# The windowed-attention loop of a fused block: look-ahead for turned pieces, another order at its end, and constant matmuls behind the first scores

## The chip, the core and the metric

The kernel runs on one core of a Trainium2 chip. The metric is the device time of one execution in microseconds (us). Engines are TensorE (PE in the profile; PEld is its weight load), VectorE (DVE), ScalarE (ACT), GpSimd (POOL) and SyncE (SP). PSUM is the memory of 8 banks of 512 float words per partition into which TensorE writes.

## What is computed

The reference is a chain of four blocks over x of shape (2, 512, 128): a hyperbolic attention block with feed-forward part (A), a quantised attention (B), a causal attention with an image token (C), and two layers of windowed attention with a gated feed-forward part (D). The change touches D alone. Its core, once for each of the 2 layers:

```python
h = shift_token(x)                      # half of the channels moved by one token
q, k, v = split(h @ wqkv)               # 8 heads of 64
q = l2norm(q) * qs
k = l2norm(k) * ksc
q, k = rotary_xpos(q, k)                # two products and a sum per element
o = local_attention(q, k, v)            # windows of 64, each sees itself and the one before
x = x + o @ wo
h = shift_token(x)
mu = h.mean(-1, keepdims=True)
var = h.var(-1, keepdims=True)
h = (h - mu) / jnp.sqrt(var + 1e-05) * lg + lb
h = h @ w1 + b1
a, g = jnp.split(h, 2, axis=-1)
x = x + (a * jax.nn.gelu(g, approximate=False)) @ w2 + b2
```

## The kernel before

Each engine's program is written out by hand, in order, and engines wait for one another's semaphores; an engine never passes an instruction that waits. The 1,024 tokens are T = 8 tiles of 128 (TB = 4 to a batch). In D a layer starts with the projection to queries, keys and values (L1762), which ScalarE copies (L674) and squares (L679); VectorE sums the squares (`norms`, L1255) and rotates the heads pair of tiles by pair of tiles (`rotate`, L1278 to L1283; keys also get their scale, L317). Keys and queries then have to be turned: a *piece* is a pair of tiles p by a group i of two 128-column blocks (i = 0, 1 keys, 2, 3 queries). TensorE turns it by four transposes (`turn_piece`, L1774) into one of two spare slots in the score banks, ScalarE copies it to SBUF (`turned_qk`, L668) and counts `qk_ev`.

The loop over u runs through UNITS = 16 units for a layer, a unit being half of the heads of one tile. In unit u TensorE turns a piece, makes the scores (`s_d`, L1799 a mask, L1810 and L1812 the products), turns the probabilities of unit u - 2 (L1859) and multiplies those of unit u - 3 with the values (`pv_d`, L1824). VectorE reduces the scores to a maximum (L1351), makes the bias (L1357) and, between, runs two steps of the rotations of later tiles (`later_rotations`, by `next(rest)`) and the reciprocal of the sums of unit u - 1 (L1369). ScalarE makes four exponentials (L698), copies the turned piece, copies the turned probabilities of unit u - 2 (L710) and, in odd units up to 11, a finished output tile (L714; later tiles are VectorE's, `put_o`, L288). GpSimd scales the probabilities (L460) and lays out values (L449, L451).

Pieces of p = 0 are turned ahead of the loop; unit u turns piece u % 4 of pair u // 4 + 1, and units 4p to 4p + 3 need all four pieces of pair p. The projection of the outputs by wo (`project_o`, L1781) of tiles 0 to 3 stands in units 12 and 13, two to a unit, of tiles 4 to 7 at the end of the loop. VectorE adds them to the residual (`add_o`, L758), sends and receives the shifted half (L1232, L1237; TensorE L1790, L1791) and normalises (`less_mean`, `variance`, `normalise`, L1313, L770, L1327); ScalarE takes the roots (`roots_d`, L662, behind a table load), and `turn_e` (L1419) and `hidden` (L1893) start the feed-forward part. `keep_busy(n)` (L1437) issues n matmuls of a constant into a bank that nobody reads then.

The waits of the unit on TensorE, which the change rewrites:

```python
if u >= 2:
    pe.wait_ge(sem["expD"], 4 * (U - 1))
    pe.wait_ge(sem["qk_ev"], UNITS * l + min(u + 3, UNITS))
if u % 4 == 0:
    pe.wait_ge(sem["qk_ev"], UNITS * l + u + 4)
if u < UNITS - 4:
    turn_piece(u // 4 + 1, u % 4, u % 2)
```

## Time and profile before

| | |
|---|---|
| median of 3 runs | 790.16 us (789.87 to 793.35) |
| the profiled execution | 788.48 us, its span 786.7 us |
| TensorE busy | 626.8 us, 80% |
| VectorE busy | 542.5 us, 69% |
| ScalarE busy | 499.9 us, 64% |
| GpSimd busy | 239.5 us, 30% |
| chain that ended last | PE 43%, DVE 30%, ACT 15%, issue 9% |

No engine is busy all the time; which of them bounds a stage differs from stage to stage. In the rows below a line of the order of time has start, duration, engine, source line and operation, what is written and read, the number of instructions merged, and in brackets how long the engine sat idle before and what it waited for. A float32 matmul counts as two instructions in some rows, so 8 of L1781 are one output projection. Times are from the start of the span.

### The profile page before, as it was taken

How to read it: one execution, taken by the hardware profiler on the slowest of the kernel's cores; microseconds unless marked ns; L12 is line 12 of the kernel's file. 1: busy time of each engine (PE TensorE's matmuls, PEld its weight loads, DVE VectorE, ACT ScalarE, POOL GpSimd, SP SyncE). 2: the span in 40 equal slices, each digit the busy share in tenths (PEclk: the TensorE clock that was granted, in tenths of full speed). 3: DMA queues.
4: the chain of work that ended last, by engine and by line, in shares of the span. 5: the costliest groups of instructions: out<-in, count | busy, mean ns of one | idle time of the engine just before them, and what ended most of it. 6: DMA issues, size and time to landing. Idle time of an engine off the chain costs nothing.

```text
span 786.7 us, 13264 instructions
## 1 busy us (share of the span) xinstructions
PE 626.8 (80%) x4802; PEld 377.4 (48%) x4802; DVE 542.5 (69%) x1119; ACT 499.9 (64%) x1187; POOL 239.5 (30%) x237
## 2 busy tenths in 40 slices
PE   7679986767789988966889798695878779578776
PEld 3312222354356655644555455543656544356654
DVE  7783328747899889767787877569754457984444
ACT  4459997661778878715477666385576439667642
POOL 5030006011789978970200000000554100055400
PEclk9779999998555555595599999896599999678999
DMA  8400000000000000000000000000000000000000
GB/s 277 157 1 1 1 1 1 0 1 0 1 2 1 1 2 2 1 1 0 1 1 2 1 1 2 1 1 0 2 2 2 1 0 0 1 2 2 1 1 27
DMA packets 9204, 9.88 MB, mean 13 GB/s; under 512 B 2890, under 2 KB 7988, under 8 KB 9012
## 3 DMA queue, kind: packets, MB, share of 16 engines
q1 hardware_dynamic: 9140, 9.04, 3.5%
q8 instruction: 39, 0.64, 0.3%
q14 instruction: 25, 0.20, 0.1%
HBM read 8.51 MB, written 0.52 MB: 11 GB/s over the span
## 4 chain that ended last, share of the span: by engine, by line
PE 43%; DVE 30%; ACT 15%; issue 9%; POOL 2%; DMA 1%; ACTq 0%; DVEq 0%; POOLq 0%
PE ps L1691 4%; PE ps L1431 4%; PE ps L1594 4%; DVE s_nmB L1086 4%; PE ps L1674 3%; ACT arena L571 3%; PE ps L1581 3%; PE ps L1711 3%; PE ps L1502 2%; ACT dev L698 2%; PE ps L1474 2%; PE ps L1893 2%; PE ps L1781 2%; ACT arena L674 2%; DVE s_nmD L1351 2%
## 5 line engine op out<-in xcount | busy, mean ns | idle before, releaser
L415 POOL TENSOR_SCALAR arena<-arena,s_rB,s_zpu 128x512 uint8<-128x512 f32 x128 | 115.9, 943 | 35.2 <-DVE s_rB L1059 34.7
L609 ACT ACTIVATE arena<-ps,s_nmB 128x512 f32<-128x512 f32 x128 | 86.6, 683 | 31.7 <-DVE s_nmB L1086 31.2
L631 ACT ACTIVATE arena<-ps,s_nmx 128x512 f32<-128x512 f32 (+3 forms) x128 | 60.7, 527 | 50.2 <-DVE s_nmx L1184 49.7
L1086 DVE TENSOR_REDUCE s_nmB<-ps 128x2 f32<-128x1024 f32 x64 | 77.3, 1216 | 6.9 <-PE ps L1581 6.6
L449 POOL COPY arena<-arena 64x512 f32<-64x512 f32 x16 | 13.0, 814 | 220.9 <-PE ps L1774 219.0
L1179 DVE TENSOR_REDUCE s_nmx<-ps 128x1 f32<-128x512 f32 (+3 forms) x128 | 56.6, 483 | 21.5 <-PE ps L1677 21.0
L571 ACT ACTIVATE arena<-ps 128x1024 f32<-128x1024 f32 x64 | 60.9, 1026 | 6.5 <-PE ps L1486 6.5
L1594 PE MATMUL ps<-cst,arena 128*128 128x128 f32 x256 | 61.0, 416 | 1.7 <-POOL arena L415 0.8
L1437 PE MATMUL ps<-ones 128*128 128x512 f16 x134 | 40.9, 457 | 24.2 <-ACT s_rn L562 3.6
L1581 PE MATMUL ps<-staged 8*128 8x512 f16 x128 | 46.7, 585 | 11.7 <-ACT arena L609 10.9
L1594 PEld LDWEIGHTS ps<-cst,arena 128*128 128x128 f32 x256 | 48.7, 218 | 14.6 <-POOL arena L415 8.0
L1691 PE MATMUL ps<-cst,arena 128*128 128x128 f32 x320 | 46.9, 301 | 8.7 <-issue 5.2
L1351 DVE TENSOR_REDUCE s_nmD<-ps 128x4 f32<-128x512 f32 x32 | 22.1, 691 | 45.7 <-PE ps L1812 30.0
L698 ACT ACTIVATE sq<-ps,s_nbD,s_dq 128x128 f32<-128x128 f32 x64 | 28.4, 454 | 33.1 <-DVE s_nbD L1357 33.1
L1691 PEld LDWEIGHTS ps<-cst,arena 128*128 128x128 f32 x320 | 39.6, 155 | 11.9 <-issue 9.6
L1762 PE MATMUL ps<-w_d,uT 128*128 128x512 f32 x96 | 42.3, 595 | 3.5 <-ACT uT L520 1.4
L1774 PE MATMUL ps<-cst,arena 128*128 128x128 f32 x128 | 26.6, 351 | 22.1 <-ACT arena L668 11.2
L1674 PE MATMUL ps<-staged 51*128 51x512 bf16 (+3 forms) x128 | 33.0, 332 | 9.8 <-ACT arena L631 8.6
L460 POOL TENSOR_TENSOR sq<-sq,s_rsD 128x512 f32<-128x512 f32 x16 | 22.4, 1400 | 51.1 <-DVE s_rsD L1369 51.1
L1437 PEld LDWEIGHTS ps<-ones 128*128 128x128 f16 x134 | 13.4, 110 | 49.2 <-issue 8.8
L698 ACT ACTIVATE dev<-ps,s_nbD,s_dq 128x128 f32<-128x128 f32 x64 | 28.5, 457 | 13.0 <-DVE s_nbD L1357 13.0
L1502 PE MATMUL ps<-arena 128*32 128x512 f32 x256 | 35.8, 633 | 1.0 <-ACT arena L571 1.0
(337 smaller groups left out, 1510.4 us busy)
## 6 DMA issues: line engine op xcount, KB each, us to landing
w_d<-in_wqkv SPq DMA_DIRECT2D x2, 768.0 KB
vec<-in_vec SPq DMA_DIRECT2D x1, 1200.0 KB, 10.8
vec<-in_vec SPq DMA_DIRECT2D x1, 960.0 KB, 8.0
w_h<-in_w SPq DMA_DIRECT2D x2, 341.0 KB
x_tok<-in_x SPq DMA_DIRECT2D x1, 512.0 KB, 4.0
arena<-in_w_f SPq DMA_DIRECT2D x2, 256.0 KB, 7.7
rope<-in_rope SPq DMA_DIRECT2D x1, 512.0 KB, 9.2
w_do<-in_wo SPq DMA_DIRECT2D x2, 256.0 KB
```

Of the source, the lines that this page charges most:

```text
L415: nc.gpsimd.tensor_scalar(u8[:, n % 4, j // 2, :, 2 * (j % 2)], prob[:, n % 2, j * 512:j * 512 + 512], sm("rB", 8)[:, c:c + 1], sm("zpu", ...
L571: nc.scalar.activation(prob[:, n % 2, half * 1024:half * 1024 + 1024], ps[:, 2 * half:2 * half + 2, :], ACT.Exp, scale=HD ** -0.5).then_in ...
L609: nc.scalar.activation(prob[:, n % 2, j * 512:j * 512 + 512], ps[:, j, :], ACT.Exp, bias=sm("nmB", 8)[:, c:c + 1], accum_out=sm("sumB", 8) ...
L631: nc.scalar.activation(probC[:, n % 2, at(qt):at(qt) + w], ps[:, bank, col:col + w], ACT.Exp, bias=nmx[:, TB * b + qt, h:h + 1]).then_inc( ...
L698: nc.scalar.activation(prob_d(U)[:, k, :], scores_d(u)[:, j, a, :], ACT.Exp, scale=sm("dq8", 8 * T)[:, h:h + 1], bias=sm("nbD", 16)[:, c:c ...
L1086: free(V.tensor_reduce(sm("nmB", 8)[:, c:c + 2], ps[:, 2 * half:2 * half + 2, :], X, ALU.max, negate=True), "maxB")
L1179: ins = V.tensor_reduce(nmx[:, TB * b + qt, h:h + 1], ps[:, bank, col:col + P * (qt + 1)], X, ALU.max, negate=True)
L1437: M(ps[:, 5, :], ones16[:, :], ones16[:, 0:1].to_broadcast([P, 512]), start=True, stop=True)
L1581: ins = M(ps[:, j, :], staged[r, G % 2, qt * P:qt * P + P], staged[r, G % 2, 512:1024], start=True, stop=True)
L1594: ins = nc.tensor.transpose(ps[:, 4 + i, c:c + P], codes[:, m % 4, i, c:c + P], ident)
L1674: M(o, stb[r, G % 2, qt * P:qt * P + P], stb[r, G % 2, 512:512 + w], start=(qt > 0), stop=False)
L1691: ins = nc.tensor.transpose(ps[:, 3 + bank, c:c + P], probC[:, n % 2, a:a + P], ident)
```

## The change

Four things are altered, all in the D loop.

1. Pieces are turned five ahead: five pieces before the loop (`FIRST_PIECES`, the fifth is piece 0 of pair 1), and unit u turns piece u + 5. The wait for ScalarE's copies is the same in each unit, u + 4, and the extra wait at u % 4 == 0 is gone. VectorE makes one rotation step more ahead of the loop, and the factors of the second half (`factors(1)`) come behind the next step.
2. Eight constant matmuls follow the scores of unit 0.
3. The projections of tiles 0 to 3 stand in unit 11 (two), 12 and 13 (one each), and VectorE's additions with them.
4. At the end, projections 4 and 5 stand in u = 17, behind the turned probabilities of unit 15 and the values of unit 14; 6 and 7 in u = 18, behind `turn_e(0)`. ScalarE loads the table of the root at u = 16, by an activation of one column.

The diff, cut to its core:

```diff
-        primed = sb("primed", [P, 12])
+        primed = sb("primed", [P, 16])
...
+        FIRST_PIECES = ((0, 2), (0, 3), (0, 0), (0, 1), (1, 0))
...
+        PROJECTED_AT = {11: (0, 1), 12: (2,), 13: (3,)}
+
+        def projected_o(t):
+
+            return ps[:, (6, 7, 0, 6)[t], 256:256 + P]
...
-                            for k, i in enumerate((2, 3, 0, 1)):
-                                turned_qk(0, i, 1 - k % 2)
+                            for k, (p, i) in enumerate(FIRST_PIECES):
+                                turned_qk(p, i, 1 - k % 2)
...
-                    if u < UNITS - 4:
-                        turned_qk(u // 4 + 1, u % 4, u % 2)
+                    if u + 5 < UNITS:
+                        turned_qk((u + 5) // PIECES, (u + 5) % PIECES, u % 2)
...
+                    if u == UNITS:
+                        load_table(ACT.Sqrt)
...
                 rest = later_rotations()
                 next(rest)
+                next(rest)
...
+                        if u == 11:
+                            add_o(0, 2, ps[:, 6:8, 256:256 + P])
                         if u in (12, 13):
-                            add_o(2 * (u - 12), 2, ps[:, 6 * (u % 2), 256:512])
+                            add_o(u - 10, 1, projected_o(u - 10).unsqueeze(1))
...
-                        if u == 0:
-                            factors(1)
                         if u == 13:
                             send(0)
                     next(rest, None)
+                    if u == 0:
+                        factors(1)
...
                         if u >= 2:
                             pe.wait_ge(sem["expD"], 4 * (U - 1))
-                            pe.wait_ge(sem["qk_ev"], UNITS * l + min(u + 3, UNITS))
-                        if u % 4 == 0:
-                            pe.wait_ge(sem["qk_ev"], UNITS * l + u + 4)
-                        if u < UNITS - 4:
-                            turn_piece(u // 4 + 1, u % 4, u % 2)
-                        if u in (12, 13):
-                            for k in range(2):
-                                project_o(2 * (u - 12) + k, ps[:, 6 * (u % 2), 256 + P * k:256 + P * k + P])
-                        if u >= 14:
-                            pe.wait_ge(sem["do_ev"], 3 * l + u - 13)
+                        pe.wait_ge(sem["qk_ev"], UNITS * l + min(u + 4, UNITS))
+                        if u + 5 < UNITS:
+                            turn_piece((u + 5) // PIECES, (u + 5) % PIECES, u % 2)
+                        for t in PROJECTED_AT.get(u, ()):
+                            project_o(t, projected_o(t))
+                        if u >= 13:
+                            pe.wait_ge(sem["do_ev"], 4 * l + u - 12)
                         if u == 14:
                             shift_rows(0)
                         s_d(u)
+                        if u == 0:
+                            keep_busy(8)
...
-                    if u >= UNITS:
-                        if u == UNITS:
-                            pe.wait_ge(sem["expD"], 4 * (U - 1))
-                            pe.wait_ge(sem["lnsq"], B * l + 1)
-                        t = TB + u - UNITS
-                        project_o(t, ps[:, 0, P * (t - TB):P * (t - TB) + P])
-                project_o(T - 1, ps[:, 0, 3 * P:4 * P])
...
+                    if u > UNITS:
+                        if u == UNITS + 1:
+                            pe.wait_ge(sem["expD"], 4 * (U - 2))
+                        else:
+                            turn_e(0)
+                        for t in range(2 * u - 2 * UNITS + 2, 2 * u - 2 * UNITS + 4):
+                            project_o(t, ps[:, 0, P * (t - TB):P * (t - TB) + P])
```

Next, what stands in a row on the engines at three places. In these rows a name behind `waits` is the semaphore.

The first place is VectorE's entry into the loop, from the last three sums of squares on. Before (L1278 to L1283 are the steps of a rotation, L1351 and L1357 belong to a unit's scores, L762 and L773 are the factors):

```order
L1255 TENSOR_REDUCE s_dss<-arena 128x16 [waits d_sq] x3
L1278 TENSOR_TENSOR o_tok<-arena,ropeL 128x1024
L1351 TENSOR_REDUCE s_nmD<-ps 128x4 [waits sD,dve_step]
L1357 TENSOR_TENSOR s_nbD<-s_nmD,s_dq 128x4 [waits dve_step]
L762 TENSOR_SCALAR s_dn<-s_dn 128x64 [waits d_n]
L773 RECIPROCAL s_dn<-s_dn 128x64 [waits dve_step]
L762 TENSOR_SCALAR s_dq<-s_dn 128x32 [waits dve_step]
L1280 TENSOR_TENSOR staged<-arena,ropeL 128x16x32 [waits d_dn]
L1281 TENSOR_TENSOR staged<-arena,ropeL 128x16x32 [waits dve_step]
L1283 TENSOR_TENSOR arena<-o_tok,staged 128x2x512 [waits dve_step]
L1351 TENSOR_REDUCE s_nmD<-ps 128x4 [waits sD,ropeQ]
```

The same place in the changed program (L1287 to L1292 the rotation, L1361 and L1369 the scores, L771 and L782 the factors):

```order
L1264 TENSOR_REDUCE s_dss<-arena 128x16 [waits d_sq] x3
L1287 TENSOR_TENSOR o_tok<-arena,ropeL 128x1024
L1289 TENSOR_TENSOR staged<-arena,ropeL 128x16x32 [waits dve_step]
L1290 TENSOR_TENSOR staged<-arena,ropeL 128x16x32 [waits dve_step]
L1361 TENSOR_REDUCE s_nmD<-ps 128x4 [waits sD,dve_step]
L1369 TENSOR_TENSOR s_nbD<-s_nmD,s_dq 128x4 [waits dve_step]
L1292 TENSOR_TENSOR arena<-o_tok,staged 128x2x512
L771 TENSOR_SCALAR s_dn<-s_dn 128x64 [waits d_n,ropeQ]
L782 RECIPROCAL s_dn<-s_dn 128x64 [waits dve_step]
L771 TENSOR_SCALAR s_dq<-s_dn 128x32 [waits dve_step]
L1287 TENSOR_TENSOR o_tok<-arena,ropeL 128x1024 [waits d_dn]
L1361 TENSOR_REDUCE s_nmD<-ps 128x4 [waits sD,dve_step]
```

The two half-width products now stand ahead of the first reduction, and the first product of the next rotation ahead of the second.

The second place is TensorE from the scores of unit 0 to those of unit 1. Before (L1812 scores, L1774 a piece turned, L1799 the mask of unit 1):

```order
L1812 MATMUL ps<-arena 64x128 x2
L1774 MATMUL ps<-cst,arena 128x128 [waits keys0]
L1774 MATMUL ps<-cst,arena 128x128 x3
L1799 MATMUL ps<-dmask,identb 128x256 x2
```

The same place changed (L1824 scores, L1449 the constant matmuls, L1786 a piece turned, L1811 the mask):

```order
L1824 MATMUL ps<-arena 64x128 x2
L1449 MATMUL ps<-ones 128x512 x8
L1786 MATMUL ps<-cst,arena 128x128 [waits ropeQ,qk_ev]
L1786 MATMUL ps<-cst,arena 128x128 x3
L1811 MATMUL ps<-dmask,identb 128x256 x2
```

Unit 1's turn is now of rotated queries, so it waits for `ropeQ`, and unit 1's scores stand behind it.

The third place is the end of the loop on TensorE, from the turned probabilities of unit 14. Before (L1859 probabilities, L1824 values, L1781 projections, L1419 the normalised tiles turned, each row ahead of an equal one with x3 or x7 left out by dots):

```order
L1859 MATMUL ps<-cst,dev 128x128 [waits ptcD,normD]
...
L1824 MATMUL ps<-arena 64x64 [waits mixD,ptcD]
...
L1781 MATMUL ps<-w_do,arena 128x128 [waits o_D1,lnsq,expD]
...
L1859 MATMUL ps<-cst,dev 128x128 [waits ptcD,normD]
...
L1824 MATMUL ps<-arena 64x64 [waits o_D1,mixD,ptcD]
...
L1781 MATMUL ps<-w_do,arena 128x128 [waits o_D1]
...
L1824 MATMUL ps<-arena 64x64 [waits mixD,ptcD]
...
L1781 MATMUL ps<-w_do,arena 128x128 [waits o_D1]
...
L1781 MATMUL ps<-w_do,arena 128x128 [waits o_D1]
...
L1419 MATMUL ps<-cst,o_tok 128x128 [waits lnD]
```

The same place changed (L1875 probabilities, L1841 values, L1793 projections, L1431 the normalised tiles):

```order
L1875 MATMUL ps<-cst,dev 128x128 [waits ptcD,normD]
...
L1841 MATMUL ps<-arena 64x64 [waits mixD,ptcD]
...
L1875 MATMUL ps<-cst,dev 128x128 [waits ptcD,normD]
...
L1841 MATMUL ps<-arena 64x64 [waits o_D1,mixD,ptcD]
...
L1793 MATMUL ps<-w_do,arena 128x128 [waits o_D1,expD]
...
L1793 MATMUL ps<-w_do,arena 128x128 [waits o_D1]
...
L1841 MATMUL ps<-arena 64x64 [waits mixD,ptcD]
...
L1431 MATMUL ps<-cst,o_tok 128x128 [waits lnD]
...
L1793 MATMUL ps<-w_do,arena 128x128 [waits o_D1]
...
L1793 MATMUL ps<-w_do,arena 128x128 [waits o_D1]
```

The probabilities of unit 15 have no projection ahead of them any more, and the turn of the normalised tiles stands ahead of the last two projections.

## Rows read from the trace of the kernel before

**Rows 1.** The page's granted clock of TensorE, in 40 slices of the span.

```profile
PEclk9779999998555555595599999896599999678999
```

**Rows 2.** Windows: stretch, busy us of PE, PEld, DVE, ACT, POOL, clock.

```profile
core 0: us, PE busy (x) PEld busy (x) DVE busy (x) ACT busy (x) POOL busy (x), PEclk, DMA share, GB/s
544.90:563.40 18.50, 11.29 (x115) 8.75 (x116) 15.69 (x26) 10.80 (x39) 7.07 (x5) 0.50 0.00 1
...
582.10:597.50 15.40, 12.69 (x205) 10.13 (x206) 3.80 (x13) 12.18 (x42) 5.97 (x7) 0.99 0.00 1
```

**Rows 3.** Order of time, VectorE: score reductions; the last two are layer 1's.

```profile
544.88 0.69 DVE L1351 TENSOR_REDUCE s_nmD<-ps 128x4 f32<-128x512 f32 x1
...
557.09 0.69 DVE L1351 TENSOR_REDUCE s_nmD<-ps 128x4 f32<-128x512 f32 x1
563.37 0.69 DVE L1351 TENSOR_REDUCE s_nmD<-ps 128x4 f32<-128x512 f32 x1 [2.22 <-PE ps L1812]
568.25 0.69 DVE L1351 TENSOR_REDUCE s_nmD<-ps 128x4 f32<-128x512 f32 x1 [1.54 <-issue]
...
582.14 0.69 DVE L1351 TENSOR_REDUCE s_nmD<-ps 128x4 f32<-128x512 f32 x1 [2.38 <-issue]
...
591.00 0.69 DVE L1351 TENSOR_REDUCE s_nmD<-ps 128x4 f32<-128x512 f32 x1 [1.83 <-ACT dev L698]
597.50 0.69 DVE L1351 TENSOR_REDUCE s_nmD<-ps 128x4 f32<-128x512 f32 x1 [5.52 <-PE ps L1812]
...
608.70 0.69 DVE L1351 TENSOR_REDUCE s_nmD<-ps 128x4 f32<-128x512 f32 x1
680.12 0.69 DVE L1351 TENSOR_REDUCE s_nmD<-ps 128x4 f32<-128x512 f32 x1
...
718.10 0.69 DVE L1351 TENSOR_REDUCE s_nmD<-ps 128x4 f32<-128x512 f32 x1 [2.58 <-issue]
```

**Rows 4.** Order of time, layer 0's front: rotation steps on VectorE, TensorE's turn in unit 2.

```profile
543.63 1.21 DVE L1278 TENSOR_TENSOR o_tok<-arena,ropeL 128x1024 f32<-128x1024 f32 x1
...
546.71 0.69 DVE L1280 TENSOR_TENSOR staged<-arena,ropeL 128x512 f32<-128x512 f32 x1
...
548.16 1.22 DVE L1283 TENSOR_TENSOR arena<-o_tok,staged 128x1024 f32<-128x1024 f32 x1
...
549.53 1.09 PE L1774 MATMUL ps<-cst,arena 128*128 128x128 f32 x4 [5.19 <-DVE arena L1283]
```

**Rows 5.** Order of time, TensorE: constant matmuls in block A, then units of layer 0.

```profile
36.36 3.57 PE L1437 MATMUL ps<-ones 128*128 128x512 f16 x8 [3.56 <-ACT s_rn L562]
...
561.50 0.63 PE L1799 MATMUL ps<-dmask,identb 128*128 128x256 bf16 x2
...
566.39 0.64 PE L1799 MATMUL ps<-dmask,identb 128*128 128x256 bf16 x2
...
579.46 1.09 PE L1774 MATMUL ps<-cst,arena 128*128 128x128 f32 x4 [2.07 <-ACT arena L668]
...
583.44 0.66 PE L1774 MATMUL ps<-cst,arena 128*128 128x128 f32 x4
```

**Rows 6.** Order of time, TensorE at unit 12: two output projections.

```profile
594.52 2.02 PE L1781 MATMUL ps<-w_do,arena 128*128 128x128 f32 x16 [1.69 <-ACT arena L668]
```

**Rows 7.** Order of time, layer 0's end of the loop, TensorE and ScalarE.

```profile
612.12 1.09 ACT L710 ACTIVATE arena<-ps 128x512 f32<-128x512 f32 x2
...
613.43 2.08 PE L1781 MATMUL ps<-w_do,arena 128*128 128x128 f32 x8
...
615.30 1.06 PE L1859 MATMUL ps<-cst,dev 128*128 128x128 f32 x4
...
616.40 0.60 ACT L710 ACTIVATE arena<-ps 128x512 f32<-128x512 f32 x1 [3.19 <-PE ps L1859]
617.02 1.28 ACT L662 ACT_TABLE_LOAD   x1
...
621.40 1.16 PE L1781 MATMUL ps<-w_do,arena 128*128 128x128 f32 x8 [1.47 <-DVE arena L288]
...
623.69 1.98 PE L1893 MATMUL ps<-uT,w_h 128*128 128x512 f32 x4 [0.69 <-ACT uT L512]
```

17 lines of the change are left out of this document (8 added, 9 removed).

## The prediction

> **What bounds the kernel now.** I read the page first for the granted TensorE clock over the span, then the D stages (two layers, some 540 to 624 us and 676 to 760 us) as a table of windows, then the list of the score reductions on VectorE, one in each unit, and last the order of time on all engines around the longest gaps between them.
>
> The page's clock line shows 5 to 6 tenths of full speed in two places, one of them the middle of each D loop's front [rows 1]. The windows say where: 0.50 (1.2 GHz) over the first four units of layer 0 and 0.99 (2.4 GHz) from unit 8 on [rows 2]. The reductions pace the loop [rows 3]. From unit 0 to unit 8 they take 37.26 us in layer 0 and 37.98 us in layer 1; from unit 8 to unit 15, 26.56 us in layer 0. Three units are long: the step to unit 4 is 6.28 us (563.37, after 557.09), to unit 8 6.54 us, to unit 12 6.50 us, against some 3 to 5 for the others. In each VectorE sits idle before the reduction (2.22, 2.38 and 5.52 us), though before the other units it is busy with the rotations until about 580 us.
>
> The reason for the three is one wait. At u = 4, 8, 12 TensorE needs the piece that was turned in the unit before and that ScalarE copies only behind that unit's four exponentials. At unit 8 TensorE is idle 2.07 us until that copy and then runs at the low level (1.09 us for four transposes) [rows 5]; at unit 12 it is idle 1.69 us and then spends 2.02 us on two output projections before the scores [rows 6].
>
> **Part A, units 0 to 8.** Pieces are turned five ahead, so the copy that unit 4 or 8 needs is made one unit of ScalarE earlier. The cover for all of it is VectorE: its rotation work is the same, so the ceiling is its idle time in this stretch, 2.22 + 1.54 + 2.38 = 6.1 us in layer 0 [rows 3]. The front costs something against it. I lay it out in layer 0's times.
>
> VectorE does the two half-width products (0.69 us each) ahead of reduction 0, so this moves from 544.88 to 546.3; ropeQ of pair 1 (the 1.22 us addition) is done at 548.4 instead of 549.4, since the factors now come behind it [rows 4]. TensorE has two turns and the scores of unit 0 done at about 542.9 (one turn, about 1.1 us, later than now: hidden, the reduction comes at 546.3). The eight constant matmuls take 3.57 us at the low level [rows 5], until 546.5; they end before 548.4, so they delay nothing, and cost nothing unless ropeQ came over 1.9 us earlier. Then TensorE turns piece (1,2), which unit 1's scores stand behind: 2.6 us at the low level, 1.5 at the high one, so reduction 1 falls at 550.6 to 551.1 where it was at 549.4. VectorE loses at most 0.5 us by this, because it has done one more rotation step by then.
>
> Reductions 2 and 3 follow at VectorE's own pace of some 3.6 us (554.2, 557.8). Here the new order has a wait of its own: piece (2,0) is turned in unit 3, not 4, and needs the scaled keys of pair 2, which VectorE finishes at about 556.5. Scores 3 are then ready at 558.1 (high level) or 559.4 (low). Scores 4 need transposes, values, one turn and scores behind these: 3.2 us at the high level, 4.9 at the low one, the latter being the distance of two units in the rows (561.50 to 566.39) [rows 5]. So reduction 4 falls between 562 and 564.4 instead of 563.4: a gain of 1.4 or a loss of 1.0 there. From unit 4 on VectorE's rotations set the pace. A unit of it is reduction and product (0.9), a reciprocal (0.2) and two rotation steps of 1.2 us, or 1.4 to 1.9 where the step is the two half-width products beside GpSimd's work: about 4.2, 4.0, 3.6, 4.0 us for units 3 to 6, then the loop's own 3.3; unit 8 comes at 577 (clock high throughout) to 579.3 (low until about 565), against 582.1. That is 2.8 to 5.1 us in layer 0, and 0.7 more in layer 1, whose front is that much longer now. I take 3.7 for each layer: the matmuls fill about 3.5 us of a gap of 5.19 [rows 4], but leave two idle stretches of 2 to 3 us, so part of the front stays at the low level.
>
> The page TensorE: Matmul & The Clock Gate of the Trainium skill (table of the two states) says that an idle engine returns to 1.2 GHz and that sustained work is needed for 2.4 GHz. By this rule the two gaps that remain would leave most of the front low and part A at its lower end, 2.8 instead of 3.7 us. The trace agrees in part: after 2.07 us idle the engine is low at 579.46, and after work without a gap it is high again at 583.44 [rows 5].
>
> **Part B, units 8 to 15.** The four projections of the first half (1.0 us each) move from two and two in units 12 and 13 to two, one, one in units 11 to 13. In layer 0's times: behind the values product that ends at 589.4 stand now projections 0 and 1 (2.0) in place of one turn (0.5), so scores 11 are ready at 592.4 and reduction 11 comes 1.45 us later than its 591.00. Then transposes 0.6, values 0.6, one projection 1.0, scores 1.0: reduction 12 at 595.65 instead of 597.50 [rows 3]. The copy that unit 12 waited for is long there. That is 1.85 us by unit 12, and unit 13 has one projection where it has two now, some 0.95 more: 2.8 us in each layer by unit 15. VectorE's additions follow the projections: one of 256 columns (0.4 us) in unit 11, one of 128 in each of 12 and 13 in place of 256; I count them at nothing, as ScalarE has until 596.6 to copy output tile 3, on which projection 3 waits. Gain 2.8 us in each layer; bounds 1.7 (only the wait of [rows 6] is saved) and 3.2.
>
> **Part C, the tail.** Now [rows 7]: ScalarE copies two units until 613.21, TensorE does projection 4 at the low level (2.08) before the transposes of unit 15 (615.30), ScalarE's last copy ends at 617.0, the table load takes 1.28 us, and the root, VectorE's normalising, the last output copy, projection 7 (621.40) and the copy of the turned tiles follow one another up to the hidden products at 623.69. After: the transposes of unit 15 stand directly behind the values product, at 613.43 to 614.4. The table load and its one-column activation run from 613.2 to 614.75 while ScalarE would be idle (3.19 us now), the last copy ends at 615.3, the root at 615.5, normalising and addition at 617.6. TensorE meanwhile: values 615.2, projections 4 and 5 at mixed levels until 617.85, the last values 618.5, the turn of the normalised tiles 619.1, the output copy on VectorE until 619.25 beside it, projections 6 and 7 until 621.1. The hidden products start at 621.1 instead of 623.69: 2.6 us, in each layer, and all behind them moves along. Bounds: 1.0 (low level for all four projections) and 3.2.
>
> **Sum.** 2 x (3.7 + 2.8 + 2.6) = 18.2 us. The profiled execution took 788.48 us (span 786.7); it becomes 770.3. The median of the runs lies 1.7 above the profiled one, so 772.0.
>
> **The rivals.**
> (1) The front gives nothing: the clock stays at the low level through units 1 to 7, each then 4.9 us on TensorE against VectorE's 4.0, and piece (2,0) waits for its keys. For it: the two remaining gaps. Against it: those units hold the same work in less idle time than now. 2 x (2.8 + 2.6) = 10.8 saved: 779.4.
> (2) The table load costs more than its row. The page ScalarE: Activation LUTs of the Trainium skill (What ACT_TABLE_LOAD costs) adds a drain of 1380 ns to the 1283 ns of the load. Worked from the rows as a mechanism of this kernel: should ScalarE be blocked about as long again as the load, the last copy comes 1.35 us later and part C shrinks to 1.25: 774.7. Against it: the load at 617.02 begins 0.02 us behind the copy and the root follows it at once.
> (3) Only the tail gains, because another wait takes the place of the copies' (projections 0 and 1 in unit 11 fully exposed, ropeQ late for each turn): 5.2 saved, 785.
> (4) Slower: the clock. Units 8 to 15 run at 0.99 now. With the waits gone TensorE waits in smaller portions; should this stretch fall to the low level, a unit costs 4.9 us [rows 5] instead of 2.95 (582.14 to 591.00 for three) [rows 3], or a little more in the odd units: about 1.8 more. Ten such units use up the whole gain of 18.2, and all 16 in both layers give 29 more: 801. Against it: its busy share rises by the change, and it kept 0.99 while 18% idle (12.69 us busy of 15.40) [rows 2].
>
> **Chances.** As forecast 0.60 (own range 767 to 777); (1) 0.20; (2) 0.08; (3) 0.07; (4) 0.05. The range of 765 to 781 holds the first three and the upper bounds of A to C. Three runs that spread by some 3 us tell 0.5% (4 us) from no change. Faster by over 0.5%: 0.91; within: 0.05; slower: 0.04.
>
> **What the new profile would show.** Steps to units 4, 8 and 12 of 4.5 us or less; no wait of TensorE's turn for ScalarE's copy at units 8 and 12; reduction 0 to reduction 8 in 32 to 33 us, reduction 8 to 15 in about 23.8; the table load in the middle of the last three copies; the first hidden product some 9.0 us after ScalarE begins the copy of unit 13's probabilities, where it is 11.6 now (612.12 to 623.69). Wrong it would be by a clock of 0.50 past unit 5, by a long wait for ropeQ or keys before a turn in units 1 to 5, or by ScalarE's last copy waiting for the load.

## The result, and the profile after

| | before | changed |
|---|---|---|
| median of 4 runs each | 790.01 us (788.75 to 793.35) | 777.47 us (776.55 to 778.91) |
| the profiled execution | 788.48 us, span 786.7 us | 776.55 us, span 774.7 us |

The changed kernel takes 0.9836 of the time (95% interval 0.9803 to 0.987), 12.5 us less. The forecast was 772.0 (765 to 781): the sign and the range hold, the size was 5.5 us too good.

The page of the changed kernel: the span, the busy times, and the granted clock of TensorE in 40 slices.

```profile
span 774.7 us, 13302 instructions
PE 623.8 (81%) x4818; PEld 378.4 (49%) x4818; DVE 544.4 (70%) x1121; ACT 501.3 (65%) x1189; POOL 236.1 (30%) x237
PEclk9779997899755555576589999989689899969989
```

The busy times are those of before within 3.4 us (GpSimd 236.1 after 239.5 us, the others 3.0 us or less), while the span is 12.0 us shorter: most of the gain is waiting that is gone. The slice in which layer 0's front lies (the 29th) has a 6 where it had a 5 [rows 1].

The D loop of layer 0 as windows: units 0 to 3, 4 to 7, 8 to 14, and from the last score reduction to the first hidden product (columns as in [rows 2]). A granted clock of 0.50 is called the low level of TensorE (1.2 GHz), 1.00 the high one (2.4 GHz); a value between is an average over a stretch with both.

```profile
547.80:566.00 18.20, 13.06 (x136) 9.69 (x136) 14.27 (x24) 10.39 (x38) 6.87 (x5) 0.65 0.01 1
566.00:580.60 14.60, 11.47 (x192) 8.78 (x192) 14.13 (x22) 10.24 (x37) 7.64 (x7) 0.97 0.01 3
580.60:605.60 25.00, 22.13 (x362) 17.58 (x362) 11.14 (x32) 20.43 (x75) 12.03 (x14) 1.00 0.01 2
605.60:618.60 13.00, 10.76 (x109) 9.46 (x110) 6.15 (x15) 7.49 (x18) 3.09 (x4) 0.74 0.00 1
```

The first four units have 0.65 where they had 0.50 [rows 2], and last 18.2 us where they lasted 18.5. Units 4 to 7 are the ones that became short: 14.6 us, after 18.8 (563.37 to 582.14, [rows 3]). The tail runs at 0.74.

The order of time on VectorE, score reductions 0, 3, 4, 7, 8, 9, 11, 12 and 15 of layer 0.

```profile
547.77 0.69 DVE L1361 TENSOR_REDUCE s_nmD<-ps 128x4 f32<-128x512 f32 x1
...
561.51 0.69 DVE L1361 TENSOR_REDUCE s_nmD<-ps 128x4 f32<-128x512 f32 x1 [1.95 <-PE ps L1824]
566.02 0.69 DVE L1361 TENSOR_REDUCE s_nmD<-ps 128x4 f32<-128x512 f32 x1 [0.96 <-DVE arena L1292]
...
578.21 0.69 DVE L1361 TENSOR_REDUCE s_nmD<-ps 128x4 f32<-128x512 f32 x1
580.60 0.68 DVE L1361 TENSOR_REDUCE s_nmD<-ps 128x4 f32<-128x512 f32 x1
584.64 0.69 DVE L1361 TENSOR_REDUCE s_nmD<-ps 128x4 f32<-128x512 f32 x1 [2.67 <-PE ps L1824]
...
592.07 0.69 DVE L1361 TENSOR_REDUCE s_nmD<-ps 128x4 f32<-128x512 f32 x1 [3.38 <-PE ps L1824]
595.39 0.69 DVE L1361 TENSOR_REDUCE s_nmD<-ps 128x4 f32<-128x512 f32 x1 [1.88 <-PE ps L1824]
...
605.57 0.69 DVE L1361 TENSOR_REDUCE s_nmD<-ps 128x4 f32<-128x512 f32 x1
```

The three long steps are gone: to unit 4 it is 4.51 us (was 6.28), to unit 8 2.39 (6.54), to unit 12 3.32 (6.50). Longer ones have come instead: 5.30 to unit 3, and 4.04 from unit 8 to unit 9.

Reductions turned out to be a poor mark at unit 8, so the account below uses the exponentials on ScalarE, in both kernels from the start of the last four sums of squares ahead of the loop. In the kernel before, layer 0, order of time: the sums of squares, the first exponential of unit 8, and that of unit 15.

```profile
539.12 4.60 DVE L1255 TENSOR_REDUCE s_dss<-arena 128x16 f32<-128x1024 f32 x4
...
583.07 0.46 ACT L698 ACTIVATE sq<-ps,s_nbD,s_dq 128x128 f32<-128x128 f32 x1 [2.88 <-DVE s_nbD L1357]
...
609.85 0.46 ACT L698 ACTIVATE dev<-ps,s_nbD,s_dq 128x128 f32<-128x128 f32 x1 [0.76 <-DVE s_nbD L1357]
```

The same three of the changed kernel, with ScalarE's end of unit 7 (its first exponential, the turned piece L675, the output tile L723).

```profile
540.56 4.60 DVE L1264 TENSOR_REDUCE s_dss<-arena 128x16 f32<-128x1024 f32 x4
...
579.37 0.46 ACT L705 ACTIVATE dev<-ps,s_nbD,s_dq 128x128 f32<-128x128 f32 x1 [1.69 <-DVE s_nbD L1369]
...
581.12 0.60 ACT L675 ACTIVATE arena<-ps 128x512 f32<-128x512 f32 x1
...
582.07 0.62 ACT L723 ACTIVATE arena<-ps 128x512 f32<-128x512 f32 x1
582.55 0.50 ACT L705 ACTIVATE sq<-ps,s_nbD,s_dq 128x128 f32<-128x128 f32 x1
...
606.72 0.46 ACT L705 ACTIVATE dev<-ps,s_nbD,s_dq 128x128 f32<-128x128 f32 x1 [0.76 <-DVE s_nbD L1369]
```

Reduction 8 begins at 580.60, but its exponentials only at 582.55: ScalarE is still busy with unit 7, whose own reduction came at 578.21. Its copies there stand behind the exponentials of unit 7, so an earlier reduction 8 does not bring them forward.

| from, to | before, layer 0 / 1 | changed, layer 0 / 1 | gain | forecast, a layer |
|---|---|---|---|---|
| sums of squares to exponential 8 | 43.95 / 44.67 | 41.99 / 41.83 | 1.96 / 2.84 | 3.7 (A) |
| exponential 8 to exponential 15 | 26.78 / 27.01 | 24.17 / 24.18 | 2.61 / 2.83 | 2.8 (B) |
| exponential 15 to first hidden product | 13.84 / 13.59 | 11.85 / 12.29 | 1.99 / 1.30 | 2.6 (C) |

That is 13.5 us over both layers. The span became 12.0 us shorter: the changed kernel's execution enters D's layer 0 1.44 us later (540.56 against 539.12) on code that the change doesn't touch, and the stretches between and behind the loops differ by 0.1 us together. Why the entry is later wasn't tested. All kernels of this study have the same code ahead of D, and in their fourteen profiles, of four sets of runs, the entry lies anywhere between 539.12 and 547.36 us. That spread is more than half of the whole gain, so the account above rests on the stretches inside the loops and not on the span.

The loop's end in the changed kernel, order of time on ScalarE and TensorE (L717 probabilities of units 13, 14 and 15, L478 table load and its activation, L669 root, L1875 turned probabilities, L1793 projections, L1431 normalised tiles, L1904 hidden products).

```profile
609.00 1.09 ACT L717 ACTIVATE arena<-ps 128x512 f32<-128x512 f32 x2
610.10 1.28 ACT L478 ACT_TABLE_LOAD   x1
610.70 1.12 PE L1875 MATMUL ps<-cst,dev 128*128 128x128 f32 x4
611.39 0.20 ACT L478 ACTIVATE primed<-ones 128x1 f32<-128x1 f16 x1
611.85 0.60 ACT L717 ACTIVATE arena<-ps 128x512 f32<-128x512 f32 x1 [0.26 <-PE ps L1875]
612.35 0.20 ACT L669 ACTIVATE s_std<-s_var 128x4 f32<-128x4 f32 x1
612.80 2.95 PE L1793 MATMUL ps<-w_do,arena 128*128 128x128 f32 x16
...
616.29 0.66 PE L1431 MATMUL ps<-cst,o_tok 128*128 128x128 f32 x4
616.78 1.95 PE L1793 MATMUL ps<-w_do,arena 128*128 128x128 f32 x16
618.57 1.88 PE L1904 MATMUL ps<-uT,w_h 128*128 128x512 f32 x4
```

The load is hidden: the last copy waits 0.26 us for TensorE's transposes, and these run at the low level (1.12 us for four). Projections 4 and 5 (x16) take 2.95 us where 6 and 7 take 1.95. The first hidden product comes 9.57 us after the copy of unit 13's probabilities; before it was 11.57 [rows 7].

### The profile page after: what moved, and what is told of

Same layout as the page of the kernel before. It is cut to its first block, busy times and chain, and to the rows that moved or that the text cites. A ratio compares the mean times of both kernels' runs of the same rounds, so it can differ in the third digit from the quotient of the medians.

```text
span 774.7 us, 13302 instructions
## 1 busy us (share of the span) xinstructions
PE 623.8 (81%) x4818; PEld 378.4 (49%) x4818; DVE 544.4 (70%) x1121; ACT 501.3 (65%) x1189; POOL 236.1 (30%) x237
## 4 chain that ended last, share of the span: by engine, by line
PE 45%; DVE 35%; ACT 10%; issue 8%; POOL 1%; DMA 1%; ACTq 0%; DVEq 0%; POOLq 0%
PE ps L1443 5%; PE ps L1703 4%; PE ps L1606 4%; DVE s_nmB L1095 4%; PE ps L1686 3%; PE ps L1723 3%; PE ps L1593 2%; PE ps L1793 2%; ACT arena L578 2%; PE ps L1841 2%; PE ps L1514 2%; PE ps L1486 2%; DVE s_nmD L1361 2%; PE ps L1904 2%; PE ps L1431 2%
## 5 line engine op out<-in xcount | busy, mean ns | idle before, releaser
L1449 PE MATMUL ps<-ones 128*128 128x512 f16 x150 | 43.4, 441 | 23.2 <-ACT s_rn L569 3.6
L1361 DVE TENSOR_REDUCE s_nmD<-ps 128x4 f32<-128x512 f32 x32 | 22.1, 690 | 34.1 <-PE ps L1824 29.8
L1774 PE MATMUL ps<-w_d,uT 128*128 128x512 f32 x96 | 42.3, 595 | 3.5 <-ACT uT L527 1.4
L705 ACT ACTIVATE sq<-ps,s_nbD,s_dq 128x128 f32<-128x128 f32 x64 | 28.5, 460 | 18.8 <-DVE s_nbD L1369 18.5
L705 ACT ACTIVATE dev<-ps,s_nbD,s_dq 128x128 f32<-128x128 f32 x64 | 28.5, 460 | 18.2 <-DVE s_nbD L1369 18.1
L1449 PEld LDWEIGHTS ps<-ones 128*128 128x128 f16 x150 | 15.0, 109 | 49.4 <-issue 8.9
L1786 PE MATMUL ps<-cst,arena 128*128 128x128 f32 x128 | 25.2, 343 | 13.6 <-DVE arena L1292 6.5
```

The source lines that it names most:

```text
L705: nc.scalar.activation(prob_d(U)[:, k, :], scores_d(u)[:, j, a, :], ACT.Exp, scale=sm("dq8", 8 * T)[:, h:h + 1], bias=sm("nbD", 16)[:, c:c ...
L1449: M(ps[:, 5, :], ones16[:, :], ones16[:, 0:1].to_broadcast([P, 512]), start=True, stop=True)
```

## The experiments

Kernels of one chip are compared with each other. On the first chip of the experiments the kernel before has a median of 798.04 us, on the second 793.93, on the third 797.39, where it was 790.01 in the result above; so ratios carry over better than times. "Units 0 to 8" is from reduction 0 to reduction 8 (in kernels with the look-ahead reduction 0 itself comes 1.45 us later behind the sums of squares, 7.21 us against 5.76, so this column shows them that much too good), "units 8 to 15" likewise, and "tail" from reduction 15 to the first hidden product, in layer 0 / layer 1.

| kernel | median | ratio, 95% interval | units 0 to 8 | units 8 to 15 | tail |
|---|---|---|---|---|---|
| before | 790.01 | | 37.26 / 37.98 | 26.56 / 26.78 | 14.99 / 14.74 |
| changed | 777.47 | 0.9836 (0.9803 to 0.987) | 32.83 / 32.67 | 24.97 / 24.98 | 13.00 / 13.44 |
| no constants | 782.0 | 0.9807 (0.9763 to 0.9851) | 32.83 / 31.51 | 24.99 / 24.99 | 12.78 / 12.23 |
| look-ahead only | 787.16 | 0.9874 (0.9834 to 0.9914) | 32.82 / 31.50 | 26.05 / 26.05 | 15.20 / 14.64 |
| end only | 793.57 | 0.995 (0.992 to 0.9979) | 37.28 / 36.42 | 29.53 / 26.62 | 12.29 / 12.26 |
| projections back | 784.33 | 0.9841 (0.9803 to 0.988) | 32.83 / 33.41 | 26.04 / 25.02 | 12.24 / 12.11 |
| changed, again | 778.76 | 0.9816 (0.9779 to 0.9853) | 32.81 / 32.67 | 24.98 / 24.98 | 13.00 / 13.43 |
| no constants, again | 778.97 | 0.9818 (0.9781 to 0.9854) | 32.83 / 32.60 | 24.97 / 24.38 | 13.00 / 12.12 |
| reciprocal first | 778.69 | 0.9809 (0.9769 to 0.9848) | 32.43 / 33.79 | 25.65 / 24.83 | 12.30 / 13.14 |
| 24 constants | 775.15 | 0.9769 (0.9732 to 0.9805) | 31.66 / 32.96 | 24.22 / 23.88 | 12.24 / 12.29 |
| 24 constants, again | 776.0 | 0.9742 (0.9712 to 0.9772) | 31.66 / 32.95 | 24.21 / 23.89 | 12.24 / 12.30 |
| gaps filled | 771.83 | 0.9685 (0.9659 to 0.9711) | 31.67 / 32.46 | 24.22 / 23.94 | 11.05 / 11.05 |
| gaps filled, reciprocal first | 775.68 | 0.974 (0.9711 to 0.9768) | 32.69 / 32.76 | 24.84 / 25.65 | 11.05 / 11.05 |
| constants alone | 796.85 | 0.9989 (0.9965 to 1.0014) | 37.26 / 37.65 | 29.47 / 26.98 | 14.95 / 15.39 |

My theory at the start: the look-ahead and the moved projections give what the front and the middle gain, the new end what the tail gains, and the eight constants nothing. The rival: the constants carry part of it through the clock.

### The four parts, one by one

Without the constants: the changed kernel less this edit.

```diff
-                        if u == 0:
-                            keep_busy(8)
```

> The changed kernel without its eight constant matmuls. Theory (the look-ahead and the order at the end carry the gain; the matmuls end 2.84 us before the turn that follows, and the turn still runs at 1.09 us, the low level): same as the changed kernel within 2 us, 776 to 779; reduction 4 of layer 0 at most 1.5 us later behind reduction 0 than the 18.2 us of the changed kernel. Rival (the clock of the front carries part A): units 2 to 5 stay at the low level in both layers, 2 to 3 us a layer, 781 to 784.

The look-ahead alone: the kernel before with edit 1 of the change (five pieces ahead, VectorE's entry), projections and end as they were. Its core on TensorE, with the copies on ScalarE and VectorE's entry left out:

```diff
-                        if u % 4 == 0:
-                            pe.wait_ge(sem["qk_ev"], UNITS * l + u + 4)
-                        if u < UNITS - 4:
-                            turn_piece(u // 4 + 1, u % 4, u % 2)
+                        pe.wait_ge(sem["qk_ev"], UNITS * l + min(u + 4, UNITS))
+                        if u + 5 < UNITS:
+                            turn_piece((u + 5) // PIECES, (u + 5) % PIECES, u % 2)
```

> The kernel before with the look-ahead alone: pieces five ahead, VectorE's order at the entry, no constant matmuls, projections and end as before. Theory: part A stays (3.0 and 3.9 us by unit 8 in the two layers) and unit 12 loses its wait of 1.7 us, less what unit 9 gives back (about 1.2): 8 to 9 us below the kernel before, 781 to 782. Rival (look-ahead gains only together with the constants): under 4 us, 786 or more.

The end alone: the kernel before with edit 4 (the root's table at u = 16, projections 4 and 5 in u = 17, 6 and 7 behind the turn of the normalised tiles). The new lines; the old projections that they replace are left out:

```diff
+                    if u == UNITS:
+                        load_table(ACT.Sqrt)
...
+                    if u > UNITS:
+                        if u == UNITS + 1:
+                            pe.wait_ge(sem["expD"], 4 * (U - 2))
+                        else:
+                            turn_e(0)
+                        for t in range(2 * u - 2 * UNITS + 2, 2 * u - 2 * UNITS + 4):
+                            project_o(t, ps[:, 0, P * (t - TB):P * (t - TB) + P])
```

> The kernel before with the order at the end of the loop and the early table load alone. Theory: from reduction 15 to the first hidden product 13.0 to 13.4 us instead of 15.0 and 14.7: 3.3 us in all, 786 to 787. Rival (my forecast of part C, low level only in part of the tail): 5.2 us, 785. Rival (the end of the loop starts later things that collide, or the load delays the last copy): no gain, 790.

The projections of tiles 0 to 3 back in units 12 and 13, two each, in the changed kernel (VectorE's additions go back with them).

```diff
-                        for t in PROJECTED_AT.get(u, ()):
-                            project_o(t, projected_o(t))
+                        if u in (12, 13):
+                            for k in range(2):
+                                project_o(2 * (u - 12) + k, ps[:, 6 * (u % 2), 256 + P * k:256 + P * k + P])
```

> The changed kernel with the first four projections two and two in units 12 and 13, as before. Theory (moving them spreads the same TensorE work; the gain of part B is the wait of the copy): reduction 8 to 15 takes 25 to 25.5 us instead of 24.97 and 24.98, 0.5 us a layer at most: 777.5 to 778.5. Rival (the spreading hides about 1 us a layer under ScalarE): 779 to 780.

Without the constants the time is 782.0 us, which is in the range that the rival named. But the kernel before takes 8 us more on this chip than in the result, and the ratio is 0.9807 against 0.9836: no gain of the constants shows. The next section compares the two on one chip.

The look-ahead is most of the change: alone 0.9874, and units 0 to 8 of layer 0 take 32.82 us, as in the changed kernel. By the exponentials it gains 1.95 and 3.99 us up to exponential 8, 1.53 and 1.77 from there to exponential 15, and nothing in the tail (-0.20 and 0.10): 9.1 us of the 13.5. The median is 10.9 us below that of the kernel before, where I expected 8 to 9.

The end alone gives 0.995 and a tail of 12.3 us, a gain of 2.7 and 2.5: part C at its forecast. My theory for that run (13.0 to 13.4 us) was wrong, and the rival right.

The moved projections give 1.07 and 1.06 us: with them back, exponential 8 to 15 takes 25.24 us in both layers, against 24.17 and 24.18. My theory for that run expected 0.5 at most; the rival, under which they matter, is right. (By reductions layer 1 seems to show nothing, 25.02 against 24.98, because reduction 8 comes late there: 33.41 us.)

The end alone shows one thing more, in the windows of units 8 to 15 of layer 0 and layer 1, which hold equal work.

```profile
590.40:619.90 29.50, 25.63 (x366) 20.56 (x366) 10.57 (x29) 18.86 (x69) 10.95 (x13) 0.88 0.00 1
726.50:753.10 26.60, 22.80 (x366) 18.11 (x366) 10.57 (x29) 18.86 (x69) 10.96 (x13) 0.99 0.01 2
```

The same instructions (x366) take 2.9 us more in layer 0, at 0.88 instead of 0.99. The low level lies in two places, each behind a wait for ScalarE's copy. The first is unit 8, behind a wait of 2.07 us: the step from reduction 8 to 9 is 4.15 us, where it is 2.88 in layer 1. The second is the two projections of unit 12:

```profile
604.14 3.65 PE L1783 MATMUL ps<-w_do,arena 128*128 128x128 f32 x16 [1.70 <-ACT arena L668]
```

This is 3.65 us where it is 2.02 in [rows 6], so the step to unit 12 is 8.1 us instead of 6.5. The kernel with constants alone (below) has the same 8.1. Both keep the waits of units 4, 8 and 12. In no profile of a kernel with the look-ahead does it occur (the two projections take 2.05 us in all of them). It may be part of why the kernel before has higher medians on these chips. A larger part may lie ahead of D, where nothing was changed: in the four profiles of this chip the entry is at 544.71 to 547.36 us, in the two of the result at 539.12 and 540.56. Neither is shown, as the kernel before was not profiled there.

### The constants, and the order on VectorE

The changed kernel once more, and the same without constants, on one chip.

> The changed kernel as it is, on the same chip as the next one, to compare the two with and without constants. Ratio to the kernel before 0.983 to 0.985. Steps from reduction 0 to reduction 8 of layer 0 again 32.83 us, the first product of the feed-forward part 12.1 to 13.4 us behind reduction 15.

> The changed kernel without the eight constant matmuls, a second time, beside the changed one. Theory (the constants end before anything that waits, and the clock is low again when the next turn starts): same median within 1.5 us, and reduction 0 to 8 of layer 0 32.83 us in both. Rival (they warm the front): 2 to 4 us slower than the changed kernel. Rival (they cost, by shifting the stretches of low clock to a worse place): 2 us or more faster.

They are 778.76 and 778.97 us, with runs that spread by 3 to 4 us: the eight constants give nothing that shows. Layer 0 is the same to exponential 8 with them and without (41.99 us each). In layer 1 the profiles without them are the shorter ones, 40.69 and 41.16 us against 41.83 in both profiles of the changed kernel; so if the constants do anything, they cost a little. The changed kernel's order of time on TensorE in the front says why: the constants, the turn in unit 1, the turned probabilities of unit 0, and the turn in unit 3.

```profile
544.03 3.07 PE L1449 MATMUL ps<-ones 128*128 128x512 f16 x8
...
549.94 1.08 PE L1786 MATMUL ps<-cst,arena 128*128 128x128 f32 x4 [2.84 <-DVE arena L1292]
...
557.13 1.12 PE L1875 MATMUL ps<-cst,sq 128*128 128x128 f32 x4 [2.77 <-POOL sq L467]
558.38 1.09 PE L1786 MATMUL ps<-cst,arena 128*128 128x128 f32 x4
```

They end at 547.1, TensorE sits idle for 2.84 us, and the turn behind runs at the low level (1.08 us), just as it does without them behind 5.84 us of idling. The next gap is 2.77 us, in unit 2, where TensorE waits for GpSimd's scaling, and the turn for unit 3 is low again (1.09). Scores 3 stand behind it, and VectorE waits 1.95 us at reduction 3. The scaling itself waits for the reciprocal, which stands behind a rotation step on VectorE. That is a rival to the clock as what holds the front back; so one kernel has the reciprocal ahead of the reduction, in units 1 to 7, without constants.

In the edit `rates(u)` is the reciprocal with its waits, moved into a function; units above 7 call it at the old place.

```diff
                 for u in range(UNITS + 1):
                     U = UNITS * l + u
+                    if 1 <= u <= 7:
+                        rates(u)
...
-                        if u == 0:
-                            keep_busy(8)
```

> The changed kernel without constants, and VectorE's reciprocal of unit u - 1 ahead of the reduction of unit u for u = 1 to 7 instead of behind it and a rotation step. Theory (in the front GpSimd, and behind it the turned probabilities, wait for this reciprocal: TensorE 2.77 us in unit 2 and 2.31 us in unit 6): 0.5 to 1.5 us less from reduction 0 to exponential 8 in each layer, 1 to 3 us faster than without it. Rival (the scores of units 1 and 3 wait for the piece's ropeQ and keys, which stay where they are, and VectorE sets the pace of the others): no difference, reduction 0 to 8 again 32.8 us.

And, apart from that, enough constants to fill most of both gaps.

```diff
-                        if u == 0:
-                            keep_busy(8)
+                        if u in (0, 2):
+                            keep_busy(16 if u == 0 else 8)
```

> The changed kernel with 16 constants behind the scores of unit 0 and 8 more behind those of unit 2, to fill the two gaps that the eight leave. Theory (VectorE's pace and the keys bind the front, the clock costs it 1 to 2 us): units 1 to 4 at the high level, reduction 3 behind reduction 0 by 12.5 us instead of 13.7, reduction 0 to 8 31.5 us: 2 us a layer faster at most. Rival (they hold up the turn and the scores behind them): slower by up to 3 us, reductions 1 and 3 later.

The reciprocal's place gives nothing (778.69 against 778.97): 0.4 less in units 0 to 8 of layer 0, 1.2 more in layer 1. My theory for it was wrong. The 24 constants give 3.6 us (775.15 against 778.76). Their order of time on TensorE: both groups of constants, and the rows that answer to those above.

```profile
544.99 4.81 PE L1449 MATMUL ps<-ones 128*128 128x512 f16 x16
550.89 0.63 PE L1786 MATMUL ps<-cst,arena 128*128 128x128 f32 x4 [1.10 <-DVE arena L1292]
...
553.74 1.91 PE L1449 MATMUL ps<-ones 128*128 128x512 f16 x8
...
557.57 0.65 PE L1875 MATMUL ps<-cst,sq 128*128 128x128 f32 x4 [1.91 <-POOL sq L467]
...
573.50 0.66 PE L1875 MATMUL ps<-cst,sq 128*128 128x128 f32 x4 [2.31 <-POOL sq L467]
574.71 1.11 PE L1786 MATMUL ps<-cst,arena 128*128 128x128 f32 x4
```

The turn takes 0.63 us, and the first four units of layer 0 15.95 us instead of 18.25. The last two rows show what is given back: in units 6 and 7 the gaps remain, and TensorE is at the low level in the turn at 574.7, so that of 2.30 us after four units 1.17 are left after eight. By the exponentials, as in the account above, the gain is 1.92 and 0.72 us to exponential 8 (40.07 and 41.11 us), nothing from there to exponential 15 (24.18 and 24.10), and 0.76 and 1.15 us in the tail (11.09 and 11.14): what the change promised for the tail (2.6) is there with these constants, 2.75 and 2.45.

### Filling what gaps remain

The 24 constants again beside the next two, and a kernel with 20 and 14 in the front and ten more at the loop's end, where they go to banks whose readers are done (`keep_busy` gets the bank as a second argument; that line is left out).

> The changed kernel with 16 constants behind the scores of unit 0 and 8 behind those of unit 2, a second time, beside the next two. Ratio to the kernel before 0.975 to 0.979.

```diff
                         s_d(u)
-                        if u == 0:
-                            keep_busy(8)
+                        if u in (0, 2):
+                            keep_busy(20 if u == 0 else 14)
+                    if u == UNITS - 1:
+                        keep_busy(2, 3)
...
+                    if u == UNITS:
+                        keep_busy(2, 1)
...
                         pv_d(t, u - 3)
+                    if u == UNITS - 1:
+                        keep_busy(6, 2)
```

> The changed kernel with 20 and 14 constants in the front and 2, 6 and 2 in the gaps of units 15 and 16, written to banks that nobody reads then. Theory (the low level of TensorE at the end of the loop costs part C about 1 us a layer): reduction 15 to the first product of the feed-forward part 11.0 to 11.5 us instead of 12.2 to 13.4, and the front as with 24 constants; 1.5 to 3 us faster than those alone. Rival (ScalarE's copies and VectorE's normalising set the end, not TensorE): 12.1 us or more, no difference.

The same with the reciprocal ahead of the reduction.

> The same as the kernel with the gaps filled, and the reciprocal ahead of the reduction in units 1 to 7. Theory (with the clock high the waits for GpSimd are what is left in the front: 1.91, 0.62, 1.76 and 2.31 us): reduction 0 to 8 under 31 us in layer 0, 1 us a layer faster. Rival (as in the kernel with the reciprocal alone, VectorE's own pace stays): same within 1 us.

And the constants without the change: the kernel before with 16 of them in unit 1 and 4 in unit 2, where its front has its gaps.

```diff
                         s_d(u)
+                        if u in (1, 2):
+                            keep_busy(16 if u == 1 else 4)
```

> The kernel before with 16 constants behind the scores of unit 1 and 4 behind those of unit 2, nothing else. Theory (the front is short of both, clock and look-ahead; with the clock high the step to unit 5 is VectorE's 4.3 instead of 4.9, and to unit 4 5.0 instead of 6.3): 2 to 4 us faster than the kernel before, the long steps to units 8 and 12 as they are (6.5). Rival (without look-ahead the three waits swallow what the clock gives): same within 1 us.

With the gaps filled it is 771.83 us, 0.9685 of the kernel before, 4.2 less than the 24 constants on the same chip: the best version of this study, and the theory, under which TensorE's level costs part C, is right (it expected 1.5 to 3 us). In the two profiles the loops give 2.9 of the 4.2, nearly all of it in the tails (1.18 and 1.25). Its windows in layer 0 are units 0 to 3, 4 to 7, and the tail; the rows below them, TensorE's order of time at the tail: the six constants, projections 4 and 5.

```profile
550.30:566.30 16.00, 13.10 (x160) 7.96 (x157) 14.59 (x25) 10.40 (x38) 6.49 (x5) 1.00 0.01 2
566.30:582.00 15.70, 12.42 (x192) 9.57 (x192) 13.98 (x21) 11.00 (x40) 9.03 (x9) 0.89 0.01 3
...
606.20:617.30 11.10, 9.87 (x117) 7.86 (x118) 6.17 (x15) 7.44 (x18) 3.15 (x4) 1.00 0.01 2
```

```profile
607.29 1.48 PE L1449 MATMUL ps<-ones 128*128 128x512 f16 x6
...
612.12 2.05 PE L1793 MATMUL ps<-w_do,arena 128*128 128x128 f32 x16
```

The tail is at 1.00 and takes 11.05 us in both layers, against 13.00 and 13.44; projections 4 and 5 take 2.05 instead of 2.95. Against the changed kernel, by the exponentials, the front gives 1.91 and 1.23 us and the tail 1.95 and 2.39, again with nothing between: 7.5 us together, in profiles of two chips.

The reciprocal ahead makes this kernel 3.85 us slower (775.68). My theory, that GpSimd's later start was worth shortening, falls. By the exponentials 3.6 us stand in the loops, 1.87 and 1.43 of them ahead of exponential 8. The profiles show two reasons. In the order of time the bias of unit 2 takes 0.53 us on VectorE,

```profile
558.96 0.53 DVE L1380 TENSOR_TENSOR s_nbD<-s_nmD,s_dq 128x4 f32<-128x4 f32 x1
```

where in the kernel with the gaps filled, in the same unit, it takes 0.16:

```profile
558.98 0.16 DVE L1369 TENSOR_TENSOR s_nbD<-s_nmD,s_dq 128x4 f32<-128x4 f32 x1
```

Those of units 1 and 3 take 0.59 and 0.71. The GpSimd scaling, released ahead of the reduction, now runs beside the bias (in unit 2 from 558.43 to 559.47), and in each of the three units the bias ends 0.02 us behind the scaling. Four exponentials wait for the bias.

The other reason is the level of TensorE. The probabilities of unit 0 now are turned at once behind the constants, so the two short waits ahead of unit 3's turn (0.60 us each, for the scaling and for the keys) have become one of 2.27 us for the keys. Behind the scores of that unit TensorE falls to the low level and stays there through units 3 and 4, busy without a gap. That the longer wait is the cause is likely, but not shown. The windows of unit 3, with the reciprocal ahead and then with the gaps filled alone:

```profile
562.35:567.24 4.89, 4.89 (x51) 3.71 (x52) 4.10 (x8) 2.86 (x11) 1.91 (x3) 0.50 0.01 2
```

```profile
562.44:566.31 3.87, 2.89 (x50) 2.22 (x50) 3.73 (x7) 2.84 (x10) 2.77 (x4) 1.00 0.00 2
```

In layer 0 units 3 and 4 are 1.02 and 0.59 us longer by it. How the 3.85 us divide between the two was not tested.

Constants alone, in the kernel before, give nothing (0.9989, 0.9965 to 1.0014), against my theory. Units 0 to 8 of layer 0 take 37.26 us with and without them. Units 0 to 2 do run at the high level now (1.00 in each window), but VectorE sets their pace (steps of 4.54, 4.29 and 3.38 us in both), and in unit 4 the turn waits for ScalarE's copy as before (0.43 us, where it was 0.25) and runs at the low level behind it, as does the rest of unit 4 (0.50). So the high level did not last up to the step to unit 5, which is 4.89 us, after 4.88. What constants in unit 3 or 4 as well would give to the kernel before was not run.

Not tried: the scores of a unit ahead of its turn, which would take the wait for keys out of reduction 3.

## Why the prediction was right, and where its sizes were off

**What bounds the kernel: right.** The wait for the piece that ScalarE copies last made the three long steps. At unit 4 it is short (TensorE idle 0.25 us in layer 0, 1.20 in layer 1, against 2.07 and 1.69 at units 8 and 12), yet the turn begins at the end of the copy in both layers, and the step is 6.28 and 6.27 us; it is 6.27 again with constants alone, where the clock ahead of it is high. With the look-ahead alone the steps to units 4 and 8 are 4.51 and 2.39, that to unit 12 is 5.24 with both projections still in it, and this is most of the gain. "No wait of TensorE's turn for the copy at units 8 and 12" and steps of at most 4.5 us to units 4, 8, 12 are what the trace has (4.51, 2.39, 3.32).

**Part A, the step that failed: "unit 8 comes at 577 to 579.3", counted at the reduction.** Less the later entry (1.44), reduction 8 comes at 579.16, at the late end of this range, and the stretch from reduction 0 is 32.83 us, as forecast (32 to 33). From the sums of squares to reduction 8 part A gained 2.98 and 3.87 us, 0.55 less in both layers together than twice 3.7. But the sum took reduction 8 as the point from which ScalarE goes on. In the new order reduction 8 overtakes ScalarE, its exponential follows only when unit 7's copies are done, and 4.04 us then pass to reduction 9. By the exponentials part A was worth 1.96 and 2.84 us, so this handover took 2.05 of the 2.6 us that are missing in A.

The forecast of the single units was also a little early. Less the same 1.44 us, reduction 3 came at 560.07 and reduction 4 at 564.58, where scores 3 were foreseen at 558.1 or 559.4 and reduction 4 at 564.4 at the latest. Two things were missed: the scaling on GpSimd takes 1.86 to 1.93 us beside the rotations of units 1 to 3, so TensorE waited 2.77 us for it in unit 2, and the turns of units 1 to 3 all ran at the low level.

With gaps of 2.84 and 2.77 us the first four units had 0.65, with these filled 1.00. By the Trainium skill (TensorE: Matmul & The Clock Gate, table of the two states) idle time returns the engine to 1.2 GHz. The trace agrees with it, and 2.8, which the prediction gave for part A by this rule, would have been the better choice than 3.7; but most of what is missing went to the handover, so 2.8 would have come close partly by luck.

**Part B: right.** 2.61 and 2.83 us against 2.8. Projections 0 and 1 in unit 11 and one each in 12 and 13 take 2.05 us and 1.16 us:

```profile
589.07 2.05 PE L1793 MATMUL ps<-w_do,arena 128*128 128x128 f32 x16
...
593.28 1.16 PE L1793 MATMUL ps<-w_do,arena 128*128 128x128 f32 x8
```

By reductions it reads as 1.6 and 1.8 (24.97 and 24.98 us, where 23.8 was forecast), since reduction 8 is early by the handover above: what it costs A in the account by exponentials, it costs B in the one by reductions. The experiments split it: 1.07 and 1.06 by the moved projections, 1.53 and 1.77 by the look-ahead, with which unit 12 no longer waits for the copy.

**Part C: mechanism right, size off in the changed kernel.** The end alone gives 2.7 and 2.5 us, the forecast 2.6. In the changed kernel's own profile it gives 1.99 and 1.30, since the clock drops at the loop's end and stays low through projections 4 and 5. "Projections 4 and 5 at mixed levels" was in the forecast; with the same order of the end the tail lasts 12.1 us in some profiles and 13.4 in others (the table), so the level is no price of the new end alone. Even the same kernel, without constants, has 12.78 us in one profile and 13.00 in the other. What sets the level there is open; that it is the level which costs, the ten constants at the end show (11.05 us in both layers).

**Sum.** 18.2 were forecast, 13.5 came in D, 2.6 missing in A, 0.2 in B and 1.9 in C. 1.5 more were lost where nothing was changed.

**The rivals.** (1) The front gives nothing: refuted; the look-ahead alone gives 0.9874 and 1.95 and 3.99 us in the front, though the low level in units 1 to 3 is what this rival said. (2) The table load costs more than its row: refuted. It begins 0.01 us behind the copy that ends at 610.09, takes 1.28 us, its activation begins at once, and the last copy waits for TensorE and not for it. The Trainium skill (ScalarE: Activation LUTs, What ACT_TABLE_LOAD costs) adds a drain to the load; this trace does not agree, for no more than 0.01 us stands on either side of the row. (3) Only the tail: refuted by the same run as (1). (4) Units 8 to 15 at the low level: they had 1.00. Stretches of low level do occur there: the long one in kernels that keep the waits (0.88, 29.5 us), a short one in layer 1 of the kernel with the gaps filled and the reciprocal first (0.67 in unit 9, units 8 to 15 in 25.65 us).

**The constants.** I costed them at nothing, which holds to what the medians tell. The choice of 3.7 leaned on them ("the matmuls fill about 3.5 us of a gap of 5.19"), and there they gave nothing. What I did not see is that more of them are worth 3.6 us on one chip (778.76 to 775.15) and 4.2 more with those at the end on another (776.0 to 771.83).

## What to carry to other kernels

Take progress on the engine that bounds the stage next: a reduction that comes 3 us earlier is worth only what the exponential behind it gains. Look also for what a shorter wait joins together: where two waits of 0.60 us became one of 2.27 us, TensorE was at its low level in the next two units. Where TensorE waits for a piece that another engine copies last in its unit, turn the piece a unit earlier; this was worth more than all else here. Then fill what gaps are left with constant matmuls, enough of them to reach near the end of the gap: eight that ended 2.84 us early gave nothing, 24 gave 3.6 us. In the kernel that still had the waits, 20 of them in units 1 and 2 gave nothing.

## What the runs showed of the hardware

The changed kernel on another chip repeats its D loop to 0.02 us: 32.83 and 32.81 us for units 0 to 8, 13.00 and 13.00 us for the tail; the kernel with 24 constants does the same. The kernel without constants does not: units 0 to 8 of layer 1 take 31.51 us in one profile and 32.60 in the other. The kernel before, however, differs by 8 us in its median between chips, and its profile was taken on one alone; and the time at which D is entered differs by 8.2 us over all profiles, with the same code ahead of it.

A float32 product of 128x512 elements takes GpSimd 1.04 us where VectorE does no rotation and 1.40 to 1.93 us beside its rotations (units 1 to 6 of the changed kernel), and VectorE's half-width product, 0.69 us alone, up to 1.41 us beside it. Beside a score reduction, which reads PSUM, the GpSimd product still takes 1.04 us; the small bias product behind that reduction (0.16 us alone) ends only 0.02 us behind GpSimd's and so takes 0.53 to 0.71 us.
